# Second attention of a decoder kernel: transposes of the probabilities in two 64-row array tiles behind the scores, query and key projections as pairs of 64 columns beside the products with the values

## The reference

```python
    def _L1_attn_ref(hidden_states, wq, wk, wv, wo, rel_bias):
        B, S, D = (2, 256, 128)
        N_HEADS, D_KV = (16, 64)
        ...
        q = shape(hidden_states @ wq)
        k = shape(hidden_states @ wk)
        v = shape(hidden_states @ wv)
        scores = jnp.einsum('bhqd,bhkd->bhqk', q, k)
        position_bias = compute_bias(rel_bias, s, s)
        scores = scores + position_bias
        attn = jax.nn.softmax(scores.astype(jnp.float32), axis=-1).astype(scores.dtype)
        out = jnp.einsum('bhqk,bhkd->bhqd', attn, v)
        out = out.transpose(0, 2, 1, 3).reshape(b, s, INNER)
        return out @ wo
    ...
    x = x + _L1_attn_ref(_layernorm(x, axis=-1), L1_attn_wq, L1_attn_wk, L1_attn_wv, L1_attn_wo, L1_attn_rel_bias)
```

## Time and profile before

| | |
|---|---|
| time, median of 3 runs | 471.5 us (470.9 to 475.05) |
| span of the profiled execution | 473.3 us; its own time is not listed apart from the three |
| PE busy | 437.0 us (92%) |
| PEld busy | 311.4 us (66%) |
| DVE busy | 361.5 us (76%) |
| ACT busy | 287.7 us (61%) |
| POOL busy | 212.3 us (45%) |
| mean granted TensorE clock | 0.978 |

### The profile page before, as it was taken

How to read it: one execution, slowest core, us unless ns; L and a number is a source line. 1 busy time by engine, 2 the same in 40 slices (tenths; PEclk the granted TensorE clock), 3 DMA queues, 4 the chain that set the end, 5 groups by cost and what they waited for, 6 DMA issues and landing times.

```text
span 473.3 us, 13124 instructions
## 1 busy us (share of the span) xinstructions
PE 437.0 (92%) x4544; PEld 311.4 (66%) x4544; DVE 361.5 (76%) x984; ACT 287.7 (61%) x684; POOL 212.3 (45%) x548
## 2 busy tenths in 40 slices
PE   8999887997789998699999999999999997998887
PEld 6555565776667777367666666666666665887756
DVE  3897659775779989777778787777787867557786
ACT  3753436874368874577777777777777776423450
POOL 5160011650123557037766668576666676440200
PEclk9999799998989999899999999999999999999989
DMA  7499936400001131000000000000000000000001
GB/s 218 76 98 100 98 39 201 156 4 1 0 2 35 44 91 35 1 1 18 3 18 3 1 17 14 3 0 0 0 0 0 2 1 2 1 3 1 1 0 46
DMA packets 15622, 15.81 MB, mean 33 GB/s; under 512 B 1348, under 2 KB 12859, under 8 KB 15579
## 3 DMA queue, kind: packets, MB, share of 16 engines
q1 hardware_dynamic: 15579, 15.24, 15.9%
HBM read 10.52 MB, written 4.72 MB: 32 GB/s over the span
## 4 chain that ended last, share of the span: by engine, by line
PE 74%; DVE 18%; ACT 4%; issue 3%; DMA 1%; POOL 0%; SPq 0%; DVEq 0%; ACTq 0%; POOLq 0%
PE bank L967 16%; PE bank L1484 12%; PE bank L1436 10%; PE bank L1359 5%; PE bank L1280 3%; PE bank L1267 3%; PE bank L1477 3%; PE bank L1355 3%; PE bank L1168 2%; PE bank L1374 2%; DVE Y L1648 1%; PE bank L972 1%; PE bank L1070 1%; PE bank L1084 1%; PE bank L1618 1%
## 5 line engine op out<-in xcount | busy, mean ns | idle before, releaser
L877 ACT ACTIVATE SN<-SN,nmx 128x512 f32<-128x512 f32 x128 | 92.7, 725 | 9.7 <-DVE nmx L2016 7.6
L967 PE MATMUL bank<-cs,SN 128*128 128x128 f32 x512 | 67.7, 275 | 3.3 <-DVE Z L2009 1.6
L967 PEld LDWEIGHTS bank<-cs,SN 128*128 128x128 f32 x512 | 57.7, 142 | 18.4 <-issue 12.5
L1436 PE MATMUL bank<-TK,TQ 64*128 64x512 f16 x384 | 52.6, 380 | 1.4 <-DVE TK L1979 1.4
L552 POOL TENSOR_TENSOR CTW<-YT 128x128 f32<-128x128 f32 x64 | 29.6, 462 | 50.9 <-DVE YT L2014 50.6
L2001 DVE CUSTOM_DVE_ANT_0 SN<-bank,strip 128x512 f32<-128x512 f32 x64 | 43.3, 677 | 1.2 <-PE bank L1436 0.6
L2016 DVE CUSTOM_DVE_ANT_0 SN<-bank,strip 128x512 f32<-128x512 f32 x64 | 43.6, 681 | 0.0
L2009 DVE COPY PTO<-bank 128x512 f32<-128x512 f32 x32 | 22.1, 691 | 21.0 <-PE bank L1484 19.2
L972 PE MATMUL bank<-ones 128*128 128x128 f32 x230 | 34.8, 310 | 1.0 <-POOL konst L400 1.0
L972 PEld LDWEIGHTS bank<-ones 128*128 128x128 f32 x230 | 32.5, 222 | 3.9 <-issue 2.5
L2009 DVE COPY Z<-bank 128x512 f32<-128x512 f32 x32 | 22.1, 691 | 16.8 <-PE bank L1484 14.3
(11 more groups left out here) (326 smaller groups left out, 965.6 us busy)
## 6 DMA issues: line engine op xcount, KB each, us to landing
bias_rows<-biasr SPq DMA_DIRECT2D x1, 4096.0 KB, 45.2
band<-bias_rows SPq DMA_DIRECT2D x1, 3072.0 KB, 11.2
wqkv<-in_twqkv SPq DMA_DIRECT2D x8, 192.0 KB, 2.7
w1s<-in_w SPq DMA_DIRECT2D x8, 128.0 KB, 2.1
w2s<-in_w SPq DMA_DIRECT2D x8, 128.0 KB, 2.1
wB<-in_wb SPq DMA_DIRECT2D x1, 753.0 KB, 6.0
wA<-in_wa SPq DMA_DIRECT2D x1, 520.0 KB, 4.7
X<-in_x SPq DMA_DIRECT2D x2, 256.0 KB, 3.3
```

The lines of the kernel that those rows point to most:

```text
L877: sc.activation(p, p, ACT.Exp, bias=nmx[:, r % RING, h:h + 1], scale=-1.0, accum_out=psm[:, r % RING, h:h + 1]).then_inc(sm["exp_ready"], 1)
L967: return nc.tensor.transpose(out_, in_, ident[0:n, 0:n])
L1436: ins = mm(bank[2 * (s % 2) + h][:, :], TQ[u][r, q_part, S * b + P * qt:S * b + P * qt + P], TK[u][r, k_part, S * b:S * b + S], start=(k = ...
```

## The change

Three things change, all in the second attention.

1. `turned` makes its transposes in two row tiles of the array. Each 128x128 transpose becomes two: of query rows 0 to 63 and of rows 64 to 127, each with 64x128 weights and 64 moving columns. The first half goes to bank 4 and the second to bank 5, for both heads, so that a bank now holds half the queries of both heads. All 16 of a step stand together, the semaphore `tt_mm` is raised twice at their end, and their start waits for both copies (`pta_ready` and `ptb_ready`). A semaphore that nobody waits for (`turn`) is raised behind these waits.
2. `turned` moves ahead of the job: scores, transposes, job, sums, products with the values.
3. `project` for queries and keys makes, for each of its three products of 128 weight columns, two of 64 columns, for the two halves of the partitions of the same bank.

The products with the values read the halves from the two banks' copies in one access. The making of `RH` moves one step later. Nothing else on ACT, DVE or POOL moves.

```diff
@@ project
-                        ins = mm(o[:, :], WP[u][:, w_part, w:w + P], YP[:, x_part, S * g:S * g + S], start=(k == 0), stop=(k == 2))
+                        for h in range(2):
+                            d = slice(TD * h, TD * h + TD)
+                            ins = mm(o[d, :], WP[u][:, w_part, w + TD * h:w + TD * h + TD], YP[:, x_part, S * g:S * g + S],
+                                     start=(k == 0), stop=(k == 2))
@@ turned
                     pe.wait_ge(sm["exp_ready"], (n - 2) * 2 + h + 1)
-                    if s >= 3:
-                        pe.wait_ge(sm[("pta_ready", "ptb_ready")[h]], n - 2)
+                    if s >= 3 and h == 0:
+                        pe.wait_ge(sm["pta_ready"], n - 2)
+                        pe.wait_ge(sm["ptb_ready"], n - 2)
+                    pe.sem_inc(sm["turn"], 1)
                     for kt in range(TG):
-                        ins = tr(bank[4 + h][:, P * kt:P * kt + P], SN[:, r % RING, h, P * kt:P * kt + P])
-                    ins.then_inc(sm["tt_mm"], 1)
+                        c = TD * (TG * h + kt)
+                        for half in range(2):
+                            q = slice(TD * half, TD * half + TD)
+                            ins = nc.tensor.transpose(bank[4 + half][:, c:c + TD], SN[q, r % RING, h, P * kt:P * kt + P], ident[q, q])
+                            if h == 1 and kt == TG - 1:
+                                ins.then_inc(sm["tt_mm"], 1)
@@ t5_step of PE: s == 1, s == 2 and turned now ahead of the job
+                if on(s, 2, last):
+                    turned(n, s)
                 job = t5_job(s, last)
...
-                if on(s, 2, last):
-                    turned(n, s)
                 if s == 3:
@@ products with the values
-                            ins = mm(bank[6][d, 0:P], TV[u][:, TG * b + kt, d], probs_t(r, h)[:, P * kt:P * kt + P],
+                            c = TD * (TG * h + kt)
+                            ins = mm(bank[6][d, 0:P], TV[u][:, TG * b + kt, d], probs_t(r)[:, :, c:c + TD],
@@ copies, ACT and DVE
-                    sc.copy(probs_t(r, 0), bank[4][:, :]).then_inc(sm["pta_ready"], 1)
+                    sc.copy(probs_t(r)[:, 0, :], bank[4][:, :]).then_inc(sm["pta_ready"], 1)
-                    vv.tensor_copy(probs_t(r, 1), bank[5][:, :]).then_inc(sm["ptb_ready"], 1)
+                    vv.tensor_copy(probs_t(r)[:, 1, :], bank[5][:, :]).then_inc(sm["ptb_ready"], 1)
@@ DVE, RH
-                if last and s == ROWS + 2:
+                if last and s == ROWS + 3:
```

More of the change, by code:

```diff
@@ L282, in build, with probs_t @@
             WO = XB
-            def probs_t(r, h):
-                return (PTE, PTO)[r % 2][:, h, :]
+            def probs_t(r):
+                return (PTE, PTO)[r % 2]
         RH = sb("RH", [P, NG, XS])
@@ L322, in build @@
             bias_mm bias_ready tw0 tw1 tw_split ld_wo ld_band strip_ready ow_ready ctw_ready
-            pj_mm pj_hi pj_ready ts_mm ttr_ready ttr_turn exp_ready rps_ready rpp_ready raw_ready tt_mm pta_ready ptb_ready tpv_mm ctt_ready wo_mm to_ready
+            pj_mm pj_hi pj_ready ts_mm ttr_ready turn exp_ready rps_ready rpp_ready raw_ready tt_mm pta_ready ptb_ready tpv_mm ctt_ready wo_mm to_ready
             rh_ready rj_mm rj_ready bs_mm m_ready as_sub as_exp as_ready ast_mm ast_ready hq_mm ast_low hq_ready mt_mm mrow_ready mb_mm nm_ready eb_ready hb_mm w0_ready f_mm
@@ L1441, in t5_step @@
                         project(2, 0, FIRST_BANKS[2])
+                if s == 1:
+                    projected_norm(1)
+                if s == 2:
+                    pe.wait_ge(sm["ln_yt"], 10)
+                    pe.wait_ge(sm["acc_ready"], 2 * NE + 2)
+                    project(3, 0, FIRST_BANKS[3])
+                    pe.wait_ge(sm["pj_hi"], 3)
+                    project(4, 0, FIRST_BANKS[4])
+                if on(s, 2, last):
+                    turned(n, s)
                 job = t5_job(s, last)
@@ L1999, in t5_step @@
                     dve.wait_ge(sm["ts_mm"], n * 2)
-                    dve.sem_inc(sm["ttr_turn"], 1)
+                    dve.sem_inc(sm["turn"], 1)
                     vv.tensor_tensor_reduce(out=SN[:, r1 % RING, 0, :], in0=bank[2 * (r1 % 2)][:, :], in1=strip[u1][:, 0, c1:c1 + S], scale=-1.0,
```

## The result

The changed kernel takes 502.5 us (median of four runs, 501.18 to 506.6), the kernel before, measured beside it, 471.2. The ratio, taken over the runs and not from the two medians, is 1.0635, with a 95% interval of 1.058 to 1.069. The direction was as forecast, the size was not: 478 had been said, with a range up to 500. One execution of the experiments, the profiled one of the last of them, ran at a lower granted clock throughout (0.837), so that its steps are longer, and is left out of that experiment's time.

What follows compares the result with a forecast made beforehand. PE was taken to bound the kernel, with a DVE loop adding time behind queries and keys. 13 rounds lose 10.1 us, other steps regain 0.7, 0.3, 1.6 and 0.9: +6.6, forecast 478 us (own range 474 to 487, overall 467 to 500).

Steps and rivals of the forecast that it cites:

- PE's own chain: PE's work between blocks of transposes: 2.68 us without a job, 3.46 with values, 3.34 with queries or keys.
- the loop: Transposes, projection, high half on ACT, then on DVE low half, score plus bias, copy of bank 5, next transposes: 4.07 us.
- 0.73: PE's extra idle time in steps behind queries and keys, beyond the 0.37 us of every step.
- The rival of the weight loads: Weight loads bound the half transposes: 0.11 us a pair, a block of 0.92, in all 502 us; chance 0.15.
- the 1.03 of the forecast: Time from scores to transposes waiting for the copy of bank 5: 0.19 plus 0.84 us.
- the 0.7: Gain in the last three steps with jobs: 11.60 us in place of 12.27.
- the 0.3: Gain in the step without a job after the last three with jobs: 3.00 us becomes 2.68.
- 6.6: Net loss forecast for the whole kernel, in us: 10.1 - 0.7 - 0.3 - 1.6 - 0.9.
- the term of `turn`: Raising the semaphore behind the waits before the transposes: 0 to 0.05 us a step, taken as 0.
- the term of the block: A step's half transposes on PE: 0.54 us in place of 0.96, at 0.057 a pair.

Runs made afterwards that it cites:

- the last of them: Half transposes at their old place, full-width projections, `RH` one step later on DVE, against the kernel before: 456.2 to 459.3 us, ratio 0.969.

## Why the prediction was wrong

*Right.* What bounds a step: PE's own chain, and behind queries and keys the loop. The idle time before the transposes is 1.07 there and 0.30 elsewhere, 0.77 beyond, where 0.73 had been said. For the move alone the terms of the loop, as measured in the changed kernel, gave 14.6 for four steps before that run, and it took 14.65; with the copy first on DVE the 1.90 disappeared. The pairs cost next to nothing in the steps (0.01); what they did at the jump is step two. The last step with a job lost its wait for `RH`: 4.43 for 5.28.

*The rival of the weight loads* gave 502, and that is where the time came out, but by coincidence, for other reasons. Sixteen loads of transposes take 0.61 from the first's start to the last's end, one takes 141 ns, so loads start (0.61 - 0.14) / 15 = 0.031 apart, and a pair, one load into each tile, takes 0.063, not 0.11. By the rule of the Trainium skill (TensorE: Matmul & The Clock Gate, section LDWEIGHTS) one load of 128 columns takes 0.107, an estimate from that page; the trace disagrees for loads of transposes in two tiles, where loads into the same tile start 0.063 apart; and the half transposes alone were worth 2.7%.

*Wrong, step one: the sizes of two terms of the cycle.* "`turn` ... 0 to 0.05; I take 0": it is 0.11 in each step, since nothing covers it between scores and transposes; without it they start 1.02 behind the scores, the 1.03 of the forecast. "The block is 0.54": it is 0.65, for a pair takes 0.063, not 0.057 (7 x 0.006 = 0.04), and the next group starts about 0.21 (0.65 - 7 x 0.063), not 0.14, behind the last pair. Both stand in all four steps, on PE's chain and in the loop: 4 x (0.11 + 0.11) = 0.87 a round with rounding, which is 15.15 - 14.28; over 13 rounds 11.3. In the three last steps with jobs it takes back the 0.7, in the next the 0.3.

*Wrong, step two: a cost that the sum lacked.* More instructions in PE's loop were counted only by the time that they take. At the two jumps of the loop PE stood for 3.14 and 3.45 us and then ran at 1.2 GHz for 3.4 us: 8.4 by the trace, 8.5 by the run without jumps. That would by itself have moved 478 to 486, and with 11.3 and 1.0 to 499. The two terms of step one alone would have made 490, above the forecast's own 474 to 487 but inside 467 to 500, where the run without jumps lies too (494.0): it is the jump that carried the time past 500.

So 6.6 + 11.3 + 8.4 + 1.0 = 27.3, where the spans differ by 26.1; the rest is -1.3 ahead of the first scores, where nothing was changed, 0.8 more gained in the first steps than forecast, and 0.4 each lost in the rounds and at the end. The mechanism was right; the forecast fell by the term of `turn`, the term of the block and the missing jump.

*What stays open.* The full-width projections in the changed kernel have 744 products from jump to jump and stall; the half transposes at the old place have 744 too and do not, and the two profiles count the same 14213 instructions. So the number alone does not draw the line there; what does was not tried.

## What to carry to other kernels

Before an instruction is moved, ask what its old place covers: here the projection hid the copy of bank 5 with the two instructions ahead of it on DVE, and at the old place the raising of a semaphore too, and all of it came onto the path when the transposes went ahead of it. Of the three parts only one was worth having: against the 175.5 us of the 13 rounds the half transposes alone took 165.5 and the move alone 190.8, and the pairs, added to the half transposes, 11.2 more, all of it at the jumps. A change that splits instructions has a price at a loop's jump that no busy time shows; look at PE's timeline at the jump, before and after. The packets of the instruction queue are a hint and no more: 26 or 28 in the kernels that jump without a pause, 46 in those with pauses, but 40 or 41 in those that are written out, which load everything and do not pause. The releaser that a row names is the last to come by the record, not always the one that counts: twice here (the exponential, the score plus bias) a run in which that engine was later, or the same, took the wait away.

## What the runs showed of the hardware

A jump back of PE cost 3.1 to 3.8 us of standing still in the four kernels whose loop was loaded again, and the granted clock was 1.2 GHz in the steps behind it (3.4 us in the changed kernel, 3 to 6 in the others); together a jump cost 3 to 7 us. 616 products and as many loads from jump to jump were kept (no packet of that queue between 258.3 and 375.3 in the kernel before), 768 were not (9 between 262 and 326 in the changed one); of the two loops with 744 one was kept (no packet between 253.5 and 362) and one was not. The Trainium skill (Runtime: NRT & Kernel Launch, section Instruction fetch mechanics) has PE's instructions in a memory of 128 KiB, filled in blocks of 16 KiB, and a taken branch to a page outside a window of two waiting for a load. Packets of 0.75 MB / 46 = 16 KB and the pause agree with it; the window of two does not: the 616 products and as many loads that were kept are nearly five blocks, an estimate from the section's 256 instructions a block.

16 half transposes in two 64-row tiles took 0.65 where 8 whole ones took 0.96. They start 0.031 apart, the whole ones 0.11; if the time goes with the columns, halves one after the other would start 0.055 apart. So the two tiles work at once, by this reckoning; no run had half transposes in one tile alone.
